# Cutting cross-quadrant block moves from eight runs a partition to one in a four-layer graph-attention kernel

## What is computed

```python
x = _layernorm(x + _L0_gnn_ref(x, adj, ...), axis=-1)   # one head, elu
x = _layernorm(x + _L1_gnn_ref(x, adj, ...), axis=-1)   # one head, elu
x = _layernorm(x + _L2_gnn_ref(x, adj, ...), axis=-1)   # eight heads, edge-type bias, out @ Wp + bp
x = _layernorm(x + _L3_gnn_ref(x, adj, ...), axis=-1)   # scores from leaky(u_i + v_j) . a, elu
```

## Time and profile before

| | us |
|---|---|
| median of 3 runs | 9005.03 |
| lowest and highest run | 9004.63, 9019.0 |
| span of the profiled execution | 9019.7 |

### The profile page before, as it was taken

One profiled execution on the slowest core, in us unless ns is written; L12 is line 12 of the kernel. 1 busy time (PEld: TensorE's weight loads), 2 busy tenths in 40 slices (PEclk: granted clock), 3 DMA queues, 4 the chain that ended last, 5 costly groups with the idle time before them and its releaser, 6 DMA issues.

```text
span 9019.7 us, 165963 instructions
## 1 busy us (share of the span) xinstructions
PE 8145.7 (90%) x58360; PEld 3645.7 (40%) x58360; DVE 7407.4 (82%) x11189; ACT 7012.7 (78%) x8204; POOL 1428.7 (16%) x582
## 2 busy tenths in 40 slices
PE   3899998989999999998999989999899998989999
PEld 1534435344353433434334353443534435343352
DVE  3788787988879878798787978878788787988878
ACT  2787786977869778797787878778687786977877
POOL 0301203021030301203012030120302103021000
PEclk7999999999999999999999999999999999999999
DMA  2714426253262623526245271442615426253251
GB/s 73 159 35 107 107 52 156 42 124 87 61 143 51 141 63 71 135 48 157 44 91 122 43 171 36 103 109 54 156 39 115 98 52 152 46 129 77 60 123 19
DMA packets 2150362, 822.71 MB, mean 91 GB/s; under 512 B 1146914, under 2 KB 2129954, under 8 KB 2147362
## 3 DMA queue, kind: packets, MB, share of 16 engines
q1 hardware_dynamic: 2149410, 810.76, 40.5%
HBM read 76.25 MB, written 4.19 MB: 9 GB/s over the span
## 4 chain that ended last, share of the span: by engine, by line
PE 38%; SPq 23%; DVE 15%; issue 13%; ACT 9%; DMA 1%; DVEq 0%; POOL 0%; ACTq 0%; POOLq 0%
SPq L381 22%; PE psum L817 21%; DVE work L1400 6%; ACT work L1043 5%; PE psum L528 3%; PE psum L600 3%; PE psum L695 2%; DVE work L1279 2%; PE psum L670 1%; DVE work L1251 1%; PE psum L523 1%; PE psum L545 1%; ACT spare L886 1%; ACT spare L881 1%; PE psum L784 1%
## 5 line engine op out<-in xcount | busy, mean ns | idle before, releaser
L817 PE MATMUL psum<-work,pick 128*32 128x512 f32 x32768 | 3766.7, 599 | 192.1 <-DVE work L1400 161.5
L1043 ACT ACTIVATE work<-spare,ucol 128x1024 f32<-128x1024 f32 x3402 | 3631.8, 1145 | 51.9 <-PE psum L817 47.3
L1400 DVE TENSOR_SCALAR work<-spare,ucol 128x1024 f32<-128x1024 f32 x4790 | 3248.9, 744 | 72.3 <-PE psum L817 55.9
L817 PEld LDWEIGHTS psum<-work,pick 128*32 128x32 f32 x32768 | 977.8, 110 | 2531.4 <-issue 2069.1
L953 ACT ACTIVATE work<-psum,beta 128x1024 f32<-128x1024 f32 x1024 | 1139.6, 1113 | 559.8 <-PE psum L670 398.5
L1251 DVE CUSTOM_DVE_ANT_0 work<-psum,work 128x1024 f32<-128x1024 f32 x1024 | 1227.0, 1198 | 247.1 <-ACT work L953 237.4
L1279 DVE STREAM_TRANSPOSE work<-work 128x1024 f32<-128x1024 f32 x960 | 1190.9, 1240 | 263.3 <-DMA work<-work 168.7
L960 ACT ACTIVATE work<-work,least 128x1024 f32<-128x1024 f32 x1024 | 1172.7, 1145 | 27.5 <-DVE least L1251 27.5
L1481 POOL TENSOR_TENSOR rstd<-rstd,neg_half 128x8 f32<-128x8 f32 x64 | 131.6, 2056 | 5024.0 <-DVE rstd L1190 5024.0
L670 PE MATMUL psum<-x_split,q_hi 128*128 128x512 f32 x2048 | 852.2, 497 | 0.0
L666 PE MATMUL psum<-mask,ident_b 128*128 128x512 bf16 x2048 | 636.7, 393 | 228.3 <-DVE least L1251 225.1
(11 more groups left out here) (167 smaller groups left out, 7053.2 us busy)
## 6 DMA issues: line engine op xcount, KB each, us to landing
work<-work SPq DMA_DIRECT2D x2560, 128.0 KB, 2.4
spare<-work SPq DMA_DIRECT2D x1280, 128.0 KB, 2.5
adj_in<-in_adj SPq DMA_DIRECT2D x128, 512.0 KB, 4.8
q_lo<-adj_in SPq DMA_DIRECT2D x1024, 64.0 KB, 2.1
q_lo<-spare SPq DMA_DIRECT2D x1024, 64.0 KB, 2.1
work<-work SPq DMA_DIRECT2D x1792, 32.0 KB, 1.9
mask<-mask_next SPq DMA_DIRECT2D x16, 2048.0 KB, 9.2
x_in<-in_x SPq DMA_DIRECT2D x16, 256.0 KB, 10.2
```

The source lines that it names most:

```text
L817: mm = pe.matmul(slot[32 * q:32 * q + 32, cols], pick[:, 15 - kk:47 - kk], ring[kk % 4][q][:, cols], start=False, stop=(kk == 15), skip_gr ...
L1043: ins = act.activation(ring[kk % 4][q], v3, ACT.Relu, bias=ucol[:, 4 * T + q, kk:kk + 1])
L1400: ins = dve.tensor_scalar(ring[kk % 4][q], v3, ucol[:, 4 * T + q, kk:kk + 1], 0.0, ALU.add, ALU.max)
```

## The change

The blocks of a buffer are stored by destination quadrant: the transpose writes block 4*b + c at place (c, b), so the 8 blocks that go from one quadrant to another are one piece of 4096 bytes (quad), 2048 (pair) or 1024 (tile) a partition. The destination is stored by source quadrant in the same way. Each of the 16 transfers of a move still carries the same bytes between the same partitions. VectorE's transposes read their source in another order (blocks 4 apart, `by_part`) and write blocks in the new order; TensorE's products read the moved data with the source quadrant as the outer step (1024, 2048 or 4096 bytes between the four pieces in place of 128, 256 or 512); the copy L1360 permutes blocks on its way. `MOVE_DONE` is 256, a name for the old number. The core of the diff:

```diff
+def by_part(rows):
+    return rows.rearrange("p (b c j) -> p c b j", c=4, j=32)

             def move(dst, src, done):
+                parts = src.rearrange("p (c y) -> p c y", c=4)
                 for turn_ in range(4):
                     for a in range(4):
                         c = (a + turn_) % 4
-                        sp.dma_start(dst[32 * c:32 * c + 32, :, a, :], src[32 * a:32 * a + 32, :, c, :]).then_inc(done, 16)
+                        sp.dma_start(dst[32 * c:32 * c + 32, a, :], parts[32 * a:32 * a + 32, c, :]).then_inc(done, 16)
...
-                    src = blocks[k % 2].rearrange("p (b c x) -> p b c x", c=4, x=P)
-                    dst = quadT[k % 3].rearrange("p (b c x) -> p b c x", c=4, x=P)
+                    dst = quadT[k % 3].rearrange("p (a y) -> p a y", a=4)
...
-                src = quadT[k % 3].rearrange("p (b a h x) -> p b a h x", a=4, h=2, x=F)
+                src = quadT[k % 3].rearrange("p (a b h x) -> p b a h x", a=4, h=2, x=F)
...
-                    dst = blocks[k % 2].rearrange("p (b h t i) -> p b h t i", h=2, t=2, i=32)
-                    dve.transpose(dst[:, :, h, half, :], probs[n % 4].rearrange("p (b j) -> p b j", j=32))\
+                    dst = blocks[k % 2].rearrange("p (c b h t i) -> p c b h t i", c=4, h=2, t=2, i=32)
+                    dve.transpose(dst[:, :, :, h, half, :], by_part(probs[n % 4]))\
                        .then_inc(s_blocks, 1)
...
-                dve.tensor_copy(tile3T, turn).then_inc(s_turn_free, 1)
+                dve.tensor_copy(tile3T.rearrange("p (a b i) -> p b a i", a=4, i=32),
+                                turn.rearrange("p (b a i) -> p b a i", a=4, i=32)).then_inc(s_turn_free, 1)
```

More of the change, by code:

```diff
@@ L55 @@
 KEEP = 16
+MOVE_DONE = 16 * 16
 SPAN = 63
@@ L380, in move @@
                         c = (a + turn_) % 4
-                        sp.dma_start(dst[32 * c:32 * c + 32, :, a, :], src[32 * a:32 * a + 32, :, c, :]).then_inc(done, 16)
+                        sp.dma_start(dst[32 * c:32 * c + 32, a, :], parts[32 * a:32 * a + 32, c, :]).then_inc(done, 16)
             def move_quads(g, more, tail):
-                ready(s_moved_a, (g * NT + NT) * 256)
+                ready(s_moved_a, (g * NT + NT) * MOVE_DONE)
                 if more:
@@ L395, in move_quads @@
                         ready(s_pv3, tail * NT + NT)
-                    src = blocks[k % 2].rearrange("p (b c x) -> p b c x", c=4, x=P)
-                    dst = quadT[k % 3].rearrange("p (b c x) -> p b c x", c=4, x=P)
+                    dst = quadT[k % 3].rearrange("p (a y) -> p a y", a=4)
                     if k == 2 and tail is not None:
                         store(tail)
-                    move(dst, src, s_moved[k % 4])
+                    move(dst, blocks[k % 2], s_moved[k % 4])
                     if more:
@@ L409, in move_pair @@
                     ready(s_pv_a, g * NT + m)
-                move(pairA_T.rearrange("p (b c x) -> p b c x", c=4, x=F),
-                     blocksA[m % 2].rearrange("p (b c x) -> p b c x", c=4, x=F), s_moved_a)
+                move(pairA_T.rearrange("p (a y) -> p a y", a=4), blocksA[m % 2], s_moved_a)
             def move_tile(g, T):
@@ L417, in move_tile @@
                     ready(s_pv3, g * NT + T)
-                move(tile3T.rearrange("p (b c x) -> p b c x", c=4, x=32),
-                     blocks3.rearrange("p (b c x) -> p b c x", c=4, x=32), s_moved3)
+                move(tile3T.rearrange("p (a y) -> p a y", a=4), blocks3, s_moved3)
             def copy_mask():
@@ L593, in pv_pair @@
                     pe.wait_ge(s_copied_a, g * 4 + m // 2)
-                pe.wait_ge(s_moved_a, (g * NT + m + 1) * 256)
-                src = pairA_T.rearrange("p (b a t i) -> p b a t i", a=4, t=2, i=32)
+                pe.wait_ge(s_moved_a, (g * NT + m + 1) * MOVE_DONE)
+                src = pairA_T.rearrange("p (a b t i) -> p b a t i", a=4, t=2, i=32)
                 cols = slice(HALF + p % 2 * 2 * P, HALF + p % 2 * 2 * P + 2 * P)
@@ L688, in pv_quad @@
                         pe.wait_ge(s_beta4, g + 1)
-                    pe.wait_ge(s_moved[k % 4], g * (MOVES[k % 4] * 256) + (moved_before(k) + 1) * 256)
-                src = quadT[k % 3].rearrange("p (b a h x) -> p b a h x", a=4, h=2, x=F)
+                    pe.wait_ge(s_moved[k % 4], g * (MOVES[k % 4] * MOVE_DONE) + (moved_before(k) + 1) * MOVE_DONE)
+                src = quadT[k % 3].rearrange("p (a b h x) -> p b a h x", a=4, h=2, x=F)
                 cols = slice(2 * tt * P, 2 * tt * P + 2 * P)
@@ L767, in pv_tile @@
                     pe.wait_ge(s_copied3, g * 2 + 1)
+                src = tile3T.rearrange("p (a b i) -> p b a i", a=4, i=32)
                 for j in range(NT):
                     half = slice(F * (j % 2), F * (j % 2) + F)
-                    mm = pe.matmul(outT[half, T % 4 * P:(T % 4 + 1) * P], values[3][:, j, :],
-                                   tile3T[:, j * P:(j + 1) * P], start=(j < 2), stop=(j >= NT - 2))
+                    dst = outT[half, T % 4 * P:(T % 4 + 1) * P].rearrange("p (a i) -> p a i", a=4)
+                    mm = pe.matmul(dst, values[3][:, j, :], src[:, j, :, :], start=(j < 2), stop=(j >= NT - 2))
                 mm.then_inc(s_pv3, 1)
@@ L828, in layer3 @@
                     if T and kk == 14:
-                        pe.wait_ge(s_moved3, (g * (NT - 1) + T) * 256)
+                        pe.wait_ge(s_moved3, (g * (NT - 1) + T) * MOVE_DONE)
                         pv_tile(g, T - 1)
@@ L1158, in blocks_a @@
                 if m % 2 == 0 and (m >= 4 or not_first(g)):
-                    dve.wait_ge(s_moved_a, (g * NT + m // 2 - 1) * 256)
+                    dve.wait_ge(s_moved_a, (g * NT + m // 2 - 1) * MOVE_DONE)
                 dve.wait_ge(s_probs_a, g * 2 * NT + m + 1)
-                dst = blocksA[m // 2 % 2].rearrange("p (b t i) -> p b t i", t=2, i=32)
-                dve.transpose(dst[:, :, m % 2, :], probsA.rearrange("p (b j) -> p b j", j=32))\
+                dst = blocksA[m // 2 % 2].rearrange("p (c b t i) -> p c b t i", c=4, t=2, i=32)
+                dve.transpose(dst[:, :, :, m % 2, :], by_part(probsA))\
                    .then_inc(s_blocks_a, 1)
@@ L1274, in turn_tile @@
                     dve.wait_ge(s_moved[(k - 2) % 4],
-                                g * (MOVES[(k - 2) % 4] * 256) + (moved_before(k - 2) + 1) * 256)
+                                g * (MOVES[(k - 2) % 4] * MOVE_DONE) + (moved_before(k - 2) + 1) * MOVE_DONE)
                 if moved:
                     dve.wait_ge(s_probs, g * TILES2 + n + 1)
-                    dst = blocks[k % 2].rearrange("p (b h t i) -> p b h t i", h=2, t=2, i=32)
-                    dve.transpose(dst[:, :, h, half, :], probs[n % 4].rearrange("p (b j) -> p b j", j=32))\
+                    dst = blocks[k % 2].rearrange("p (c b h t i) -> p c b h t i", c=4, h=2, t=2, i=32)
+                    dve.transpose(dst[:, :, :, h, half, :], by_part(probs[n % 4]))\
                        .then_inc(s_blocks, 1)
@@ L1352, in blocks_tile3 @@
                 if T:
-                    dve.wait_ge(s_moved3, (g * (NT - 1) + T) * 256)
+                    dve.wait_ge(s_moved3, (g * (NT - 1) + T) * MOVE_DONE)
                 dve.wait_ge(s_probs3, g * NT + T + 1)
-                dve.transpose(blocks3.rearrange("p (b i) -> p b i", i=32),
-                              probs3[T % 2].rearrange("p (b j) -> p b j", j=32)).then_inc(s_blocks3, 1)
+                dve.transpose(blocks3.rearrange("p (c b i) -> p c b i", c=4, i=32), by_part(probs3[T % 2]))\
+                   .then_inc(s_blocks3, 1)
             def copy_tile3(it):
                 filled(dve, it, ("tile3", 0))
-                dve.tensor_copy(tile3T, turn).then_inc(s_turn_free, 1)
+                dve.tensor_copy(tile3T.rearrange("p (a b i) -> p b a i", a=4, i=32),
+                                turn.rearrange("p (b a i) -> p b a i", a=4, i=32)).then_inc(s_turn_free, 1)
             def out3(g, it):
```

## The result

| | before | after |
|---|---|---|
| median us | 9008.75 (4 runs, 9004.63 to 9019.0) | 8904.01 (4 runs, 8889.56 to 8915.81) |
| span of the profiled execution, us | 9019.7 | 8903.0 |
| ratio of the runs | | 0.9879 (95% interval 0.9865 to 0.9893) |

The kernel is 1.2% faster, 104.7 us by the medians. The forecast was 125 us.

What follows compares the result with a forecast made beforehand. SP's queue issuing the sixteen transfers of a move (L381) was taken to bound quads 2 to 14. 120 us there plus 5 in the prologue, off the 9005.03 median, gave 8880 us; range 8790 to 9010.

Steps and rivals of the forecast that it cites:

- the prologue: Before the main stretches: 8 pair moves x 16 x 0.050 = 6.4 us, nine tenths setting the end, so 5 us gained.
- the moves hardly count elsewhere: Outside quads 2 to 14: in layer 3 TensorE is busy 268.24 of 280 us; only the prologue was excepted.
- The price of an issue: SP's L381 transfers: one run instead of eight makes an issue 50 ns shorter, 613 to 563 ns; bounds 14 and 273.
- The pairs of rows: Profiled loads with eight runs against one: 64 partitions 635 against 597 ns (38 less), 128 partitions 413 against 338 (75 less).
- the sum: Whole kernel: quads 2 to 14 give 16 x 7.5 = 120 us, the prologue 5, together 125 us less.
- The part that comes out: Quads 2 to 14: of SP's 10.4 us saved per graph, 7.5 us shortens the stretch.
- the cap: Quads 2 to 14: TensorE's 139.40 busy us plus 7.1 waiting for VectorE make 146.5, so at most 8.3 us falls.
- The data term: Moves' data: longer runs make a 128 KB transfer about 0.09 us cheaper; left out of the sum, bounds 0 and 8 us.
- No effect of the runs: Rival: SP's issue does not depend on runs; only landings improve, up to 25 us, 8980 to 9003 us; chance 0.15.
- The fall to adj_in's 338 ns: Rival: SP's issue falls to 338 ns and TensorE sets the pace, 8778 to 8837 us; chance 0.13.
- Slower transposes: Rival: VectorE's transposes read stepped blocks more slowly; 9775 us at doubled duration, 9130 at 0.7 us more each; chance 0.12.
- The edits that I cost at nothing: Other pair and tile moves, VectorE's transposes, TensorE's products and the copy L1360: each taken as 0 us.

Runs made afterwards that it cites:

- e1_quads: Changed kernel with only layer 2's quads laid out by quadrant, pairs and tiles as in the old kernel; 8912.94 us, ratio 0.9887.
- e2_pairs_tiles: Changed kernel with only pairs and tiles laid out by quadrant, quads as in the old kernel; 8998.62 us, ratio 0.9984.
- e3_source_only: Old kernel with only the source buffers of moves laid out by quadrant, destination and products as before; 9012.02 us, ratio 1.0006.
- e4_destination_only: Old kernel with only the destination buffers of moves laid out by quadrant, source and transposes as before; 9008.02 us, ratio 0.9996.
- e9_changed_again: The changed kernel unaltered, run again for comparison; 8892.75 us, ratio 0.9878.
- e10_loads_later: Changed kernel with the input loads behind quads 2, 3 and 4 moved behind later quads, same issues in another order; 8897.38 us, ratio 0.9887.
- e6_four_issues: Changed kernel with each quad moved by 4 transfers of 128 partitions within their quadrants instead of 16, results wrong; 8810.31 us, ratio 0.9780.

## Why the prediction was right, and where its steps were off

**The place was right.** SP's queue set the pace in quads 2 to 14, and the gain came from there: 85.4 of the 104.7 us, and `e1_quads` alone has 0.9887. Pairs and tiles with the prologue bring some 10 us (`e2_pairs_tiles`). The statement that the moves hardly count elsewhere was a little off: outside the stretches (span less their sum) the four profiled kernels with eight-run quads (before, `e2_pairs_tiles`, `e3_source_only`, `e4_destination_only`) take 6529 to 6547 us, and the four with one-run quads (after, `e1_quads`, `e9_changed_again`, `e10_loads_later`) 6514 to 6516. `e1_quads` has the old pairs and tiles, so these 13 to 33 us come with the quads too. Some 18 us of them lie between layer 2's last product and layer 3's first transposes; what makes them is not shown.

**The price of an issue was mis-sized: 50 ns were taken, and the median fell by 22, the mean of the quads by 36.** The pairs of rows were good analogues for an issue after a pause: the 128-partition pair gave 75, and it fell by 78. The step that failed is that I applied this to issues in a row. The earlier trace rows held a hint: minimum 585 and median 613, so issues in a row were already held back by something other than themselves. The 10.4 us a graph of the sum were 7.5. An undisturbed quad, 10.47 us before and 10.03 after, would have given 13 x 0.44 = 5.7 us.

**The part that comes out was right, its reason was not.** The sum let 7.5 of 10.4 us come out because of a cap; 5.3 of 7.5 came out, the same share. But the cap was too low. It took TensorE's 7.1 us of waits for VectorE as independent of the moves and said 8.3 us; `e6_four_issues` gained 11.3 us a graph and has 2.7 us of these waits left, so most of them were late effects of the moves: VectorE's transposes wait for a landing, its L1251 comes behind them, and TensorE waits for that. What did not come out shows in SP's own queue: the time between its issues grew by 1.6 us a graph, with waits for VectorE's transposes where none were before, and the last landing of a stretch came 0.4 us later after its issue. That the forecast is only 20 us off is in part luck: the stretches gave 35 us less than the 120 of the sum, and some of that came back outside them, where the sum had nothing.

**The data term was too hopeful, and rightly left out.** I put 0.09 us a transfer as its likely gain, from 227 to 269 GB/s. The stretch before gives 199/0.87 = 229 GB/s at full share, the stretch after 207/0.87 = 238: 0.02 us. The mask copy's 269 was no good analogue: it stays in its own partitions, as `e6_four_issues` does, which has 380. The rule cited from the Trainium skill ("DMA: Bandwidth & Descriptors", "Why small descriptors are slow (HBM only)"), that SBUF transfers don't suffer from small descriptors, is by these numbers nearly right for 512 bytes against 4096: the rate differs by 4%.

**The prologue gave less than 5 us.** At 10.39 less 10.01 us for a move, eight moves can bring 3.0 us, and in the traces the first quad's move starts only 1 us earlier (277.0 us against the 278.0 of the earlier trace rows). The working also rounds down: nine tenths of 6.4 are 5.8.

**The rivals.** No effect of the runs: refuted, 507 and 591 against 585 and 613. The fall to adj_in's 338 ns: did not happen. Slower transposes: refuted. Transposes into quads, and products of quads, in the changed kernel (against the earlier trace rows):

```profile
L1284 DVE STREAM_TRANSPOSE work<-work x960: 1231/1240/1247, 268.9 to 8590.7; 128x1024 f32<-128x1024 f32 x192
...
L699 PE MATMUL psum<-work,vw x5120: 379/379/690, 291.6 to 8602.4; 128*64 128x256 f32 x197
```

The transposes into tiles have 1239 ns where 1237 stood, the tiles' products 273 and the copy out of PSUM 1220 as before. The edits that I cost at nothing cost nothing.

## What to carry to other kernels

When a queue that issues DMAs sets the pace, price an issue in a row, not after a pause: the length of an undisturbed burst, divided by its count, is the number that multiplies. Here both sides of a transfer had to be contiguous before a longer run was worth anything, and the layout that makes them so was free, with pieces of 128 bytes or more left in a row to the other engines; smaller pieces were not tried. Before cutting issues further, look at the DMA share of the same stretch: here half the issues met the data's limit at once.

## What the runs showed of the hardware

- An issue from SP has a cost after a pause and a rate in a row, and the two do not move together: 585 and 613 ns (medians) with eight runs of 512 bytes, 585 and 597 with two runs, 507 and 591 with one, for 32 partitions. In the changed kernel the rate is the same for 128 KB and 64 KB. What sets it stays open.
- A transfer with one contiguous side is cut as if it had none: 2150362 packets, against 430042 with both sides contiguous.
- With 64 partitions (256 KB) an issue costs 461 ns after a pause and 936 in a row, at 0.93 DMA share.
- Between runs of 512 and 4096 bytes the data rate across quadrants hardly changes (GB/s divided by the DMA share): 229 GB/s with 512 bytes, 238 with 4096, and 222 for 64-partition transfers. The same bytes kept in their own partitions, with all 128 in a transfer, ran at 380.
- Loads issued from a second queue ran into moves in flight: the landings of the quads into `spare` went from 2.4 to 3.0 us. One such wait of TensorE, 2.38 us, was followed by half the granted clock: sixteen products took 3.45 us in place of 1.95.
